# A recommendation tower on one core: lookup ids spread by TensorE into PSUM, and two chunks of each table made by ScalarE

## What is computed

```python
e = jnp.stack([tbl_0[ids[:, 0]], ..., tbl_25[ids[:, 25]]], axis=1)
all_emb = jnp.concatenate([bottom_output[:, None, :], e], axis=1)   # 512 x 27 x 128
gram = jnp.einsum('bfd,bgd->bfg', all_emb, all_emb)
z = gram[:, _TRIU_I, _TRIU_J]                                      # 512 x 351
h = jnp.concatenate([z, r_bottom_output], axis=1)
h = jnp.maximum(h @ W_top1 + b_top1, 0.0)                          # 479 -> 512
h = jnp.maximum(h @ W_top2 + b_top2, 0.0)                          # 512 -> 256
y = h @ W_top3
```

## Time and profile before

| what | us |
|---|---|
| median of 3 runs | 123.95 (123.61 to 126.53) |
| the profiled execution, its time | 124.74 |
| the profiled execution, its span | 122.7 |
| TensorE (PE) busy | 95.8 |
| VectorE (DVE) busy | 52.1 |
| ScalarE (ACT) busy | 47.7 |
| GpSimd (POOL) busy | 80.5 |

### The profile page before, as it was taken

The page is one execution under the profiler, slowest core; times in us unless marked ns, Lnnn a source line. Parts: engine busy times, 40 slices in busy tenths (PEclk is TensorE's granted clock), DMA queues, the critical chain, the costliest instruction groups (busy, mean ns, idle before and its releaser), DMA issues.

```text
span 122.7 us, 2459 instructions
## 1 busy us (share of the span) xinstructions
PE 95.8 (78%) x960; PEld 81.3 (66%) x960; DVE 52.1 (42%) x101; ACT 47.7 (39%) x69; POOL 80.5 (66%) x81
## 2 busy tenths in 40 slices
PE   5937799999989984935551749829996957999992
PEld 5926578888868864924441639719984946789891
DVE  2039899999999912522040014105033114211121
ACT  4154899898995522332100300410331321312212
POOL 2779888988897878787777778787877774023000
PEclk9999999999999999997568555996799999999999
DMA  2689999999999522138321247322247422053100
GB/s 34 228 255 240 248 238 257 253 257 241 235 279 237 155 80 69 48 79 154 101 66 43 68 88 142 99 64 51 64 82 134 112 56 60 5 87 57 36 0 1
DMA packets 19696, 15.35 MB, mean 125 GB/s; under 512 B 13957, under 2 KB 15873, under 8 KB 19685
## 3 DMA queue, kind: packets, MB, share of 16 engines
q1 hardware_dynamic: 14898, 10.09, 35.1%
q0 software_dynamic: 2416, 4.82, 15.7%
q10 hardware_dynamic: 2370, 0.29, 1.6%
HBM read 13.70 MB, written 1.49 MB: 124 GB/s over the span
## 4 chain that ended last, share of the span: by engine, by line
POOL 62%; issue 17%; PE 13%; DMA 4%; POOLq 2%; DVE 1%; ACT 1%; SPq 0%
POOL mixed_sb L344 54%; POOL side_sb L336 7%; PE banks L489 4%; PE banks L496 4%; DMA mixed_sb<-in_mixed_table,mixed_rows_sb 2%; PE banks L483 2%; POOLq L348 2%; DMA side_ids_sb<-in_side_ids 2%; PE banks L503 1%; PE banks L451 1%; PE banks L430 1%; DVE hidden L616 1%; SPq L364 0%; ACT hidden L670 0%; ACT y_sb L609 0%
## 5 line engine op out<-in xcount | busy, mean ns | idle before, releaser
L344 POOL DMA_INDIRECT mixed_sb<-in_mixed_table,mixed_rows_sb x64 | 68.8, 1074 | 19.5 <-issue 19.5
L626 DVE TENSOR_SCALAR one_hot<-lookup_ids_sb,starts_sb 125x512 fp32r<-125x512 int32 x60 | 25.6, 491 | 5.9 <-DMA lookup_ids_sb<-in_lookup_ids 5.7
L430 PE MATMUL banks<-identity,mixed_sb 128*128 128x128 f32 x64 | 11.9, 313 | 19.3 <-DMA mixed_sb<-in_mixed_table,mixed_rows_sb 19.2
L413 PE MATMUL banks<-one_hot,high 125*128 125x512 f32 x60 | 24.1, 402 | 3.6 <-DVE low L640 2.8
L415 PE MATMUL banks<-one_hot,low 125*128 125x512 f32 x60 | 23.5, 391 | 0.0
L430 PEld LDWEIGHTS banks<-identity,mixed_sb 128*128 128x128 f32 x64 | 7.9, 155 | 22.6 <-DMA mixed_sb<-in_mixed_table,mixed_rows_sb 22.0
L451 PE MATMUL banks<-turned 128*56 128x52 f32 x512 | 18.3, 233 | 0.0
L451 PEld LDWEIGHTS banks<-turned 128*56 128x56 f32 x512 | 16.5, 148 | 2.5 <-issue 2.0
L577 DVE COPY turned<-banks 128x512 f32<-128x512 f32 (+1 forms) x7 | 4.4, 634 | 27.2 <-PE banks L430 27.2
L413 PEld LDWEIGHTS banks<-one_hot,high 125*128 125x128 f32 x60 | 11.3, 188 | 7.0 <-issue 4.5
L577 ACT COPY turned<-banks 128x512 f32<-128x512 f32 (+1 forms) x10 | 6.2, 616 | 23.2 <-PE banks L430 23.2
(11 more groups left out here) (32 smaller groups left out, 74.6 us busy)
## 6 DMA issues: line engine op xcount, KB each, us to landing
raw<-in_tbl SPq DMA_DIRECT2D x6, 448.0 KB
lookup_ids_sb<-in_lookup_ids SPq DMA_DIRECT2D x8, 256.0 KB, 7.4
raw<-in_tbl SPq DMA_DIRECT2D x2, 560.0 KB
products_dram<-products SPq DMA_DIRECT2D x12, 91.0 KB
mixed_sb<-in_mixed_table,mixed_rows_sb POOLq DMA_INDIRECT x64, 7.3
pairs<-products_dram SPq DMA_DIRECT2D x16, 39.0 KB
w_sb<-in_w SPq DMA_DIRECT2D x2, 256.0 KB
w_sb<-in_w SPq DMA_DIRECT2D x1, 512.0 KB, 15.9
```

Of the source, the lines that this page charges most:

```text
L344: pool.indirect_dma_start(mixed_sb[:, n, :], None, mixed_table, bass.IndirectOffsetOnAxis(ap=mixed_rows_sb[:, n:n + 1], axis=0),).then_inc ...
L413: pe.matmul(lookup_ps[:, i % 2, :], high[0:TABLE_PARTS, i % 2, c, :], columns, start=(c == 0), stop=False)
L430: last = pe.transpose(turn_ps[:, n % 2, k, :], source, identity[:])
L626: dve.tensor_scalar(one_hot[0:TABLE_PARTS, n % ONE_HOT_RING, :], lookup_ids_sb[0:TABLE_PARTS, i % RAW_RING, :], float(-c), starts_sb[0:TAB ...
```

## The change

The ids of a table are no longer loaded onto all partitions. One DMA on ScalarE's queue brings all eight rows of ids, 8 x 1512 integers, of which the last 1000 columns are a selection matrix made on the host. ScalarE converts them to fp32r (`ids_rows`). For each table TensorE multiplies the 125 selection columns of this table with the 512 ids, which puts the table's ids on 125 partitions of a PSUM bank. It does so twice (`spread_ids`), once into a bank that VectorE reads and once into one that ScalarE reads. The banks are the four that the products use later. The first two tables are spread ahead of the plan, table i + 1 at the start of lookup i. SyncE's queue loses the eight loads of ids and the waits ahead of five of them.

ScalarE makes two chunks of each table in place of one, VectorE 6 or 8 in place of 7 or 9. The identity multiplications become 8 ahead of the spread and 4 behind it, in the banks of the transposes, and VectorE clears 32 rows of the four product banks, which they used to fill.

```diff
-SCALAR_CHUNKS_OF = [1] * len(LOOKUP)
+SCALAR_CHUNKS_OF = [2] * len(LOOKUP)
...
+WARM_UPS = (8, 4)
...
+UNUSED_ROWS = slice(32, 64)
...
+VECTOR_IDS_BANKS, SCALAR_IDS_BANKS = [2, 3], [4, 5]
+ID_COLUMNS = BATCH + len(LOOKUP) * TABLE_PARTS
...
-            def load_lookup_ids(i):
-                sp.dma_start(lookup_ids_sb[:, i % RAW_RING, :], lookup_ids[i:i + 1, :].to_broadcast([P, BATCH])
-                             ).then_inc(lookup_ids_in[i], 16)
...
-                sp.wait_ge(one_hot_set, FIRST_VECTOR[i - RAW_RING + 1])
-                sp.wait_ge(distance_set, FIRST_SCALAR[i - RAW_RING + 1])
-                load_lookup_ids(i)
...
+            def spread_ids(i):
+
+                for bank in (VECTOR_IDS_BANKS[i % 2], SCALAR_IDS_BANKS[i % 2]):
+                    last = pe.matmul(banks[0:TABLE_PARTS, bank, :],
+                                     ids_rows[:, BATCH + i * TABLE_PARTS:BATCH + (i + 1) * TABLE_PARTS],
+                                     ids_rows[:, 0:BATCH], start=True, stop=True)
+                last.then_inc(ids_spread, 1)
+
             def lookup(i):
+                if 1 <= i < len(LOOKUP) - 1:
+                    spread_ids(i + 1)
...
-            for bank in PRODUCT_BANKS:
-                for k in range(BANK // P):
-                    pe.matmul(banks[:, bank, k * P:(k + 1) * P], identity[:], identity[:], start=True, stop=True)
+            for _ in range(WARM_UPS[0]):
+                pe.matmul(turn_ps[:, 0, 0, :], identity[:], identity[:], start=True, stop=True)
+            pe.wait_ge(ids_rounded, 1)
+            pe.wait_ge(banks_cleared, 1)
+            spread_ids(0)
+            spread_ids(1)
+            for _ in range(WARM_UPS[1]):
+                pe.matmul(turn_ps[:, 0, 0, :], identity[:], identity[:], start=True, stop=True)
...
-                                  lookup_ids_sb[0:TABLE_PARTS, i % RAW_RING, :],
+                                  banks[0:TABLE_PARTS, VECTOR_IDS_BANKS[i % 2], :],
                                   float(-c), starts_sb[0:TABLE_PARTS, kind:kind + 1],
                                   ALU.add, ALU.is_equal).then_inc(one_hot_set, 1)
...
-                dve.wait_ge(lookup_ids_in[i], 16)
+                dve.wait_ge(ids_spread, i + 1)
...
+            dve.memset(banks[UNUSED_ROWS, PRODUCT_BANKS[0]:PRODUCT_BANKS[-1] + 1, :], 0.0
+                       ).then_inc(banks_cleared, 1)
...
-                    act.activation(distance[0:TABLE_PARTS, :], lookup_ids_sb[0:TABLE_PARTS, i % RAW_RING, :],
+                    act.activation(distance[0:TABLE_PARTS, :], banks[0:TABLE_PARTS, SCALAR_IDS_BANKS[i % 2], :],
...
+            act.dma_start(ids_raw[:], lookup_ids).then_inc(lookup_ids_in, 16)
+            act.wait_ge(lookup_ids_in, 16)
+            act.copy(ids_rows[:], ids_raw[:]).then_inc(ids_rounded, 1)
             round_table(0)
```

More of the change, by code:

```diff
@@ L240, in dlrm_tower @@
         side_ids_sb = sb("side_ids_sb", [P, TILES, SIDES], I32)
-        lookup_ids_sb = sb("lookup_ids_sb", [P, RAW_RING, BATCH], I32)
+        ids_raw = sb("ids_raw", [len(LOOKUP), ID_COLUMNS], I32)
+        ids_rows = sb("ids_rows", [len(LOOKUP), ID_COLUMNS], F32R)
         identity = sb("identity", [P, P])
@@ L271, in dlrm_tower @@
         starts_in, mixed_ids_in, side_ids_in = sem("starts_in"), sem("mixed_ids_in"), sem("side_ids_in")
-        lookup_ids_in = [sem(f"lookup_ids_in_{i}") for i in range(len(LOOKUP))]
+        lookup_ids_in, ids_rounded, ids_spread = sem("lookup_ids_in"), sem("ids_rounded"), sem("ids_spread")
         table_in = [sem(f"table_in_{i}") for i in range(len(LOOKUP))]
         dense_in, dense_spread, w1_in, w2_in, small_in = sem("dense_in"), sem("dense_spread"), sem("w1_in"), sem("w2_in"), sem("small_in")
+        banks_cleared = sem("banks_cleared")
         ones_set, identity_set, padding_set = sem("ones_set"), sem("identity_set"), sem("padding_set")
@@ L366, in _ @@
             load_table(0)
-            load_lookup_ids(0)
             sp.dma_start(dense_turned[:], dense).then_inc(dense_in, 16)
@@ L680, in make_one_hots @@
             def make_one_hots(i):
-                act.wait_ge(lookup_ids_in[i], 16)
+                act.wait_ge(ids_spread, i + 1)
                 if i >= 2:
@@ L755 @@
     side_ids = ids[:, SIDE].reshape(TILES, P, SIDES).transpose(1, 0, 2).reshape(P, TILES * SIDES)
+    chosen = np.eye(len(LOOKUP), dtype=ids.dtype).repeat(TABLE_PARTS, axis=1)
+    lookup_ids = np.concatenate([ids[:, LOOKUP].T, chosen], axis=1)
     starts = np.zeros((P, FIRST_START + FIRST_SCALAR[-1]), np.float32)
@@ L770 @@
         arg("side_ids", side_ids), [arg(f"tbl_{f}", tables[f]) for f in SIDE],
-        arg("lookup_ids", ids[:, LOOKUP].T), [arg(f"tbl_{f}", tables[f]) for f in LOOKUP],
+        arg("lookup_ids", lookup_ids), [arg(f"tbl_{f}", tables[f]) for f in LOOKUP],
         arg("mixed_ids", mixed_ids), arg("mixed_table", np.concatenate([tables[f] for f in MIXED])),
```

## The result

The changed kernel takes 117.61 us (median of 4 runs, 117.29 to 117.95) against 124.53 for the kernel before in its comparison: ratio 0.947, interval 0.939 to 0.955. The profiled execution took 117.49 us with a span of 115.6. I had forecast 118.0 and gave 83% to faster.

The account below looks back on a forecast made before the run. GpSimd's 72 indirect DMAs plus a fixed tail bound the kernel. Waits of 9.9 us fall to 3.4 (3.2 at `low`, 0.24 first gather): 124.74 - 6.5 = 118.2, forecast 118.0 against the median, range 115.3 to 121.8.

Parts of the forecast that it names:

- The bound and the cause: GpSimd's 72 indirect DMAs set the time; VectorE's `low` and one-hots from SBUF cost them 9.7 us.
- The one-hots' 3.4 us: On GpSimd: one-hots reading ids from PSUM stop delaying gathers, saving 3.4 us, range 0 to 3.4.
- VectorE's pace: One-hots from PSUM take 0.75 us, 0.67 between starts; a table of 8 chunks 5.15, of 10 chunks 6.8.
- The stalls by `low`: On GpSimd: eight `low` still delay gathers by 0.4 us each, 3.2 in all, within 0.8 to 7.6.
- GpSimd's start doesn't move: At the kernel's start: mixed gathers are released ahead of the memset, so GpSimd begins at the same time.
- The tail: Behind GpSimd's last awaited gather: last blocks, last two parts and their layers stay at 19.4 us.
- The loads of ids cost nothing on the chain: Dropping eight loads, 2 MB, frees DMA engines that nothing on the chip waits for.
- The start and the lookups' end: First ids spread at 6.1 us, first `low` at 7.0; lookups end at 52, 7 later but hidden, cost 0.
- the cover: In TensorE's waits for gathers behind the lookups: 2 to 3 us remain to hide the later lookups' end.
- The bad places of `low`: Rival: every `low` meets a gather's start near its beginning, about 0.95 us each; gain 2 to 4, time 121.5; 14%.
- freed altogether: Rival: no gather on GpSimd is held up by `low` any more; gain about 9.7 us, time 115.0; 10%.
- The slow clock in the lookups: Rival: TensorE runs the lookups at half clock, ending at about 85 us; time 145 us; 5%.

Follow-up runs that it names:

- low_from_psum: The changed kernel with the subtraction that makes `low` replaced by copies from PSUM, so its sums are not right: 116.03 us.
- psum_only: The changed kernel with one chunk of each table on ScalarE again, ids still in PSUM: 122.63 us, ratio 1.003 to the kernel before.
- sbuf_same_pace: The changed kernel with VectorE copying ids to SBUF, making one-hots from there, plus filling copies to hold the pace: 123.02 us, ratio 1.002 to the kernel before.
- warm_ups_16: The changed kernel with 14 identity multiplications ahead of the spread and 8 behind it, in place of 8 and 4: 118.0 us.
- two_chunks_only: The kernel before with two chunks of each table on ScalarE, ids still in SBUF: 122.17 us, ratio 0.992 to the kernel before.
- ids_loads_back: The changed kernel with the eight loads of ids to all partitions put back, into tiles that nothing reads: 119.24 us.
- pace_630: The changed kernel with two more VectorE copies of 512 columns from PSUM per table, ahead of its last one-hot: 119.74 us.
- pace_550: The changed kernel with one more VectorE copy of 400 columns from PSUM per table, ahead of its last one-hot: 121.39 us.

## Why the prediction was right

**The bound and the cause** held. GpSimd's sequence is the chain, and the two kinds of instruction of VectorE that the timelines pointed to are the ones that hold it up: low_from_psum takes away the waits at `low`, psum_only those beside one-hots, and sbuf_same_pace brings the latter back.

**The one-hots' 3.4 us** held. No gather beside a one-hot from PSUM takes over 0.95. Of the 3.4 one wait of 0.26, of the gather of 40.06, belongs to a `low`, so the one-hots' share was nearer 3.1. What one costs follows the same rule as `low`: in the earlier trace rows six stand 0.41 apart from 9.70, so the gather of 11.00 starts in the one of 10.93 and waits 0.34, until that one gives way at 11.34.

**VectorE's pace** held: one-hots of 0.744 (0.75 forecast), 0.66 from start to start (0.67), 5.08 us for a small table (5.15) and 6.67 for a large one (6.8).

```profile
L638 DVE TENSOR_SCALAR one_hot<-banks,starts_sb x52: 741/744/753, 6.2 to 49.8; 125x512 fp32r<-125x512 f32 x52
```

**The stalls by `low`** were the mis-sized term: 3.2 forecast, 1.5 measured. I had worked out 0.1 at VectorE's pace of 5.15 us and 0.4 at ScalarE's of 5.4, and took 0.4 for each. ScalarE didn't set the pace: its second chunk added 1.36 (25.52 to 26.88) and not 1.5, and it even waited for TensorE's results. So five small tables got the 0.1 that the sum had worked out, the first one 0.26, and the two large ones 0.36 and 0.44 against 0.5. Behind one-hots from PSUM a held gather also ends 0.90 after `low` gives way, where the prediction's steps count from the 1.0 of the kernel before.

```profile
25.52 0.67 ACT L703 ACTIVATE distance<-banks,starts_sb 125x512 f32<-125x512 f32 x1
...
26.88 0.69 ACT L703 ACTIVATE distance<-banks,starts_sb 125x512 f32<-125x512 f32 x1
```

**"GpSimd's start doesn't move"** was wrong. The release of the mixed gathers indeed didn't move, but the first gather waits for the side ids, and these landed 0.6 later, at 4.08 in place of 3.44. Runs with the new loads have 3.99 to 4.15 when they keep their order and their warm-ups (4.62 in warm_ups_16), two_chunks_only has 3.22 with the old ones. That the new DMA of ids stands in the way is likely but wasn't tried by itself. The two errors, +0.6 here and -1.7 at `low`, leave GpSimd 7.6 us earlier where I had 6.5. The tail is 0.4 longer, and the time 0.4 under the forecast. The mechanism was right, but that the time came this near is in part luck, since the two errors partly cancel.

**The loads of ids cost nothing on the chain** was wrong too, as ids_loads_back shows: about 1.3 us of GpSimd's time hang on them, mainly by way of one `low`.

**The start and the lookups' end** held: first ids spread at 6.2 (6.1 forecast), `low` at 7.25 (7.0), lookups ending at 52.1 (52), TensorE's next wait at the end of the catching up:

```profile
52.10 0.38 PE L437 MATMUL banks<-identity,side_sb 128*128 128x128 f32 x2
...
66.03 0.66 PE L437 MATMUL banks<-identity,mixed_sb 128*128 128x128 f32 x4 [2.55 <-DMA mixed_sb<-in_mixed_table,mixed_rows_sb]
```

The wait of 2.55 us is the cover that I had put at 2 to 3, and in pace_630, ten us later, it is gone.

**The rivals.** The bad places of `low` came about in psum_only (0.75 each) and pace_550 (0.57 each), so it was a real danger and a matter of half a us of pace: those two kernels took 122.63 and 121.39 us. GpSimd wasn't freed altogether: 1.5 us of waits stayed, and low_from_psum shows 116.03 us without them. The slow clock in the lookups appeared for 4 us at their start and cost nothing.

**The two pages that the prediction drew on.** By the Trainium skill, SBUF — State Buffer (Who interferes with whom), a VectorE instruction with at most one SBUF input contends with GpSimd only in a two-port mode, and whoever issues first then holds the ports that both share for the whole instruction. The traces agree: gathers wait up to 0.36 beside one-hots from SBUF and not at all beside those from PSUM. The same section of the Trainium skill infers that `tensor_tensor` leaves descriptor generation alone. The runs disagree: with the subtraction gathers are held up for as long as 1.09 in psum_only and 0.97 in ids_loads_back, and in low_from_psum, without it, none is. The Trainium skill, VectorE: DVE Perf Modes (Why PSUM operands drop a tier), has fp32 from PSUM in the slower mode. The trace agrees, with 0.66 from start to start against 0.41; here the slower instruction is the better one.

## What to carry to other kernels

When GpSimd's indirect DMAs are the chain, look at what VectorE runs at the moment each of them starts. An instruction that reads SBUF fast can cost more than a slower one that reads PSUM, and its price depends on where it falls between the gathers' steps and not on how much work VectorE has. So judge such an edit by the pace that it leaves, measure the parts together, and expect that a small edit beside it can undo the gain.

## What the runs showed that I had not expected

- GpSimd's sequence locks to VectorE's. 0.48 us more work per table costs 3.2 us at GpSimd's end and 1.2 us more costs nothing (97.66 and 94.57 against 94.50).
- Leaving out 2 MB of loads is worth 1.3 us on a chain that never waits for them, mostly because table 1 arrives in time for its `low` to miss a gather.
- Without `low` in the way, 1.4 us at the start of the sequence reach its end as 1.3. With it, starts earlier by 1.1 and 1.2 gave 0.8 and 1.3 at the end.
